# Edge features in one transfer of 128 rows, even and odd tiles, indices three chunks at a time, a written-out SyncE pass

## What is computed

```python
xn = _layernorm(x)
f1 = feature1 @ w_f1a @ w_f1b * gate_edge            # feature1: 54 per edge, gate_edge: 256 per edge
h1 = segment_sum(xn[src] * f1, dst, num_segments=N)
f2 = f1 * gate_edge
h2 = segment_sum(xn[src] * f2, dst, num_segments=N)
...
x = x + gnn(h1, h2, xn) + mix(xn)
x = x + ffn(_layernorm(x))                            # graph attention over 131072 other edges, 4 experts
```

## Time and profile before

| | us |
|---|---|
| median of 3 runs | 1259.7 |
| lowest and highest run | 1254.82, 1261.76 |
| the profiled execution's own time | 1261.14 |
| span of that execution | 1259.1 |
| mean granted TensorE clock | 0.895 of full speed |
| PE busy | 1008.7 (80%) |
| DVE busy | 780.3 (62%) |
| POOL busy | 575.8 (46%) |
| edge pass, first to last filter | 89 to 612 us of the span |

### The profile page before, as it was taken

One profiled execution on the slowest core, in us unless ns is written; L12 is line 12 of the kernel. 1 busy time (PEld: TensorE's weight loads), 2 busy tenths in 40 slices (PEclk: granted clock), 3 DMA queues, 4 the chain that ended last, 5 costly groups with the idle time before them and its releaser, 6 DMA issues.

```text
span 1259.1 us, 14085 instructions
## 1 busy us (share of the span) xinstructions
PE 1008.7 (80%) x3958; PEld 561.8 (45%) x3958; DVE 780.3 (62%) x1487; ACT 420.2 (33%) x832; POOL 575.8 (46%) x578
## 2 busy tenths in 40 slices
PE   4838796978887788888899949858879849969996
PEld 3724342333333333333344438535546525546664
DVE  5636476758667586676568775126546535656388
ACT  3324453544454454453421232121202111212241
POOL 6334656556665656555100000627675735743011
PEclk9968898989989888998999966969889969979998
DMA  9525655656656566566400101000100001011002
GB/s 222 163 64 161 196 180 168 191 181 199 194 180 193 163 191 187 166 192 185 126 34 0 3 19 10 5 2 6 37 6 4 5 3 37 5 4 3 1 16 65
DMA packets 121538, 118.62 MB, mean 94 GB/s; under 512 B 41727, under 2 KB 108939, under 8 KB 121483
## 3 DMA queue, kind: packets, MB, share of 16 engines
q1 hardware_dynamic: 98698, 72.42, 19.7%
q0 software_dynamic: 22784, 45.57, 14.0%
HBM read 112.47 MB, written 5.46 MB: 94 GB/s over the span
## 4 chain that ended last, share of the span: by engine, by line
PE 40%; DVE 23%; another core or an unknown queue 17%; issue 13%; ACT 3%; DVEq 2%; DMA 1%; POOL 1%; SPq 0%; ACTq 0%
PE psum L831 7%; PE psum L960 6%; PE psum L950 5%; PE psum L818 5%; DVE psum L1392 4%; PE psum L929 3%; DVE x_rows L1826 2%; DVE high L1396 2%; DVE high L1702 2%; DVE high L1400 2%; PE psum L864 2%; DVE parts L1692 2%; PE psum L871 2%; PE psum L938 2%
## 5 line engine op out<-in xcount | busy, mean ns | idle before, releaser
L625 POOL DMA_INDIRECT high<-xn_rows,srci x336 | 318.8, 949 | 244.7 <-PE psum L831 105.2
L831 PE MATMUL psum<-high 128*64 128x512 f32 x672 | 212.1, 679 | 4.5 <-issue 3.2
L818 PE MATMUL psum<-filter_weights,shared 54*128 54x256 f32 x672 | 120.3, 440 | 95.0 <-DVE high L1400 75.0
L661 POOL DMA_INDIRECT high<-source_rows,high x104 | 108.4, 1042 | 113.4 <-DVE high L1665 84.1
L960 PE MATMUL psum<-high 128*125 128x256 f32 x640 | 153.1, 396 | 8.8 <-ACT high L1186 6.8
L950 PE MATMUL psum<-xT,high 128*128 (+1 forms) x320 | 144.2, 594 | 10.1 <-issue 10.1
L818 PEld LDWEIGHTS psum<-filter_weights,shared 54*128 54x128 f32 x672 | 71.3, 202 | 180.4 <-DVE high L1400 101.7
L1392 DVE TENSOR_TENSOR psum<-psum,high 128x1024 f32<-128x1024 f32 x96 | 104.8, 1092 | 74.9 <-remote 42.1
L1121 ACT ACTIVATE high<-high 128x1024 f32<-128x1024 f32 x96 | 91.2, 950 | 165.0 <-DVE high L1396 104.9
L960 PEld LDWEIGHTS psum<-high 128*125 128x125 f32 x640 | 126.7, 198 | 36.3 <-ACT high L1186 8.9
L663 POOL DMA_INDIRECT high<-dest_rows,high x104 | 111.6, 1074 | 33.2 <-issue 33.2
(11 more groups left out here) (274 smaller groups left out, 1252.3 us busy)
## 6 DMA issues: line engine op xcount, KB each, us to landing
high<-in_ea SPq DMA_DIRECT2D x48, 896.0 KB
shared<-in_ea SPq DMA_DIRECT2D x96, 108.0 KB
high<-xn_rows,srci POOLq DMA_INDIRECT x336
high<-in_w SPq DMA_DIRECT2D x8, 512.0 KB
x_rows<-in_x SPq DMA_DIRECT2D x5, 448.0 KB
xn_rows<-low SPq DMA_DIRECT2D x5, 448.0 KB
out_rows<-x_rows SPq DMA_DIRECT2D x5, 448.0 KB
high<-source_rows,high POOLq DMA_INDIRECT x104
```

The lines of the kernel that those rows point to most:

```text
L625: pool.indirect_dma_start(gath[j % DEPTH][:, t, :], None, xn_rows_d, bass.IndirectOffsetOnAxis(ap=srci[:, j, t:t + 1], axis=0)).then_inc(s ...
L661: pool.indirect_dma_start(sources[b][:, t, :], None, source_rows_d, bass.IndirectOffsetOnAxis(ap=index[b][:, 0, t:t + 1], axis=0)).then_in ...
L818: ins = pe.matmul(bank[2 + s // 2][:, C * (s % 2):C * (s % 2) + C], feat[j % 2][r:r + 54, slot, :], wf[r:r + 54, :], start=True, stop=True)
L831: ins = pe.matmul(bank[j % 2][g, :], sel[j % 2][:, t, :], msgs[j % DEPTH][:, t, :], start=(t < 2), stop=(t >= CT - 2), skip_group_check=True)
```

## The change

Four edits, all in the edge pass.

1. Features: for chunks 0 to 45 one transfer of 128 rows of 2 KB takes the place of the two of 54 rows. Its source is written as 2 blocks (384 elements apart) of 64 rows of 512 elements: rows 0 to 63 get tiles 0 to 3 of 64 feature rows, rows 64 to 127 tiles 3 to 6. Rows 54 to 63 and 118 to 127 hold values that nothing reads. The last two chunks keep two transfers, now of 54 rows of 2 KB.
2. Halves: the first half of a chunk is tiles 0, 2, 4, 6, the second tiles 1, 3, 5 (before: 0 to 3, and 4 to 6). `filters`, `sums`, the gathers, ACT's square and DVE's three products follow.
3. Indices: one transfer loads the indices of three chunks into one of two halves of `srci`; SP issues it in chunks 2, 5, 8, ..., and POOL waits for indices once in three chunks.
4. SP's pass is written out over all 48 chunks; its addresses are constants.

```diff
-IDX = 6
+IDX3 = 3
+IDX = 2 * IDX3
+TILES = (range(0, CT, 2), range(1, CT, 2))
+HALVES = (slice(0, CT, 2), slice(1, CT, 2))
...
             with sp.Fori(0, npass) as p:
-                with sp.Fori(0, NCH // IDX) as i:
-                    for j in range(IDX):
-                        q = p * NCH + i * IDX + j
-                        c = i * IDX + j
-                        sp.wait_ge(filters_multiplied, q * 2 + 2)
-                        ft = ea54[bass.ds(c, 1)].rearrange("o f t p -> (o f) t p")
-                        for r, first, part in ((0, 0, slice(0, 2)), (64, 1, slice(1, 3))):
-                            sp.dma_start(feat[j % 2][r:r + 54].rearrange("f (a b) p -> f a (b p)", b=2),
-                                         ft[:, first:first + 6, :].rearrange("f (a b) p -> f a b p", b=3)[:, :, part, :]
-                                         .rearrange("f a b p -> f a (b p)")).then_inc(features_loaded[j % 2], 16)
-                        sp.wait_ge(messages_summed, q * 2 + 2)
-                        a = (j + AHEAD) % IDX
-                        sp.dma_start(srci[:, a, :], src[bass.ds(c + AHEAD, 1)].rearrange("o p t -> (o p) t")
-                                     ).then_inc(indices_loaded[a], 16)
-                        sp.dma_start(gate[j % DEPTH], ea256[bass.ds(c, 1)].rearrange("o p (t c) -> (o p) t c", t=CT)
-                                     ).then_inc(gate_loaded[j % DEPTH], 16)
+                for c in range(NCH):
+                    sp.wait_ge(filters_multiplied, p * (2 * NCH) + (2 * c + 2))
+                    if c < NCH - 2:
+                        sp.dma_start(fraw[:, FT * P * (c % 2):FT * P * (c % 2) + FT * P],
+                                     bass.AP(ea54.tensor, 54 * CT * P * c, [[3 * P, 2], [CT * P, 64], [1, FT * P]])
+                                     ).then_inc(features_loaded[c % 2], 16)
+                    else:
+                        for r in range(2):
+                            sp.dma_start(feat[c % 2][64 * r:64 * r + 54], ea54[c][:, 3 * r:3 * r + FT, :]
+                                         ).then_inc(features_loaded[c % 2], 16)
+                    sp.wait_ge(messages_summed, p * (2 * NCH) + (2 * c + 2))
+                    if c % IDX3 == IDX3 - 1:
+                        indices((c // IDX3 + 1) % (NCH // IDX3))
+                    sp.dma_start(gate[c % DEPTH], ea256[c].rearrange("p (t c) -> p t c", t=CT)
+                                 ).then_inc(gate_loaded[c % DEPTH], 16)
...
-                        pool.wait_ge(indices_loaded[j], (p * (NCH // IDX) + i) * 16 + 16)
-                        for h, tiles in enumerate((range(0, 4), range(4, CT))):
+                        if j % IDX3 == 0:
+                            pool.wait_ge(indices_loaded[j // IDX3], (p * (NCH // IDX) + i) * 16 + 16)
+                        for h, tiles in enumerate(TILES):
...
-                for t, r, slot in (((0, 0, 0), (2, 64, 0), (1, 0, 1), (3, 64, 1)),
-                                   ((4, 0, 3), (5, 64, 2), (6, 64, 3)))[h]:
-                    s = t + h
+                for t, r in (((0, 0), (4, 64), (2, 0), (6, 64)),
+                             ((1, 0), (3, 64), (5, 64)))[h]:
+                    s = (t // 2, t // 2 + 5)[h]
...
-                for t in (range(0, 4), range(4, CT))[h]:
-                    g = slice(WIN * (t % 2), WIN * (t % 2) + WIN)
+                for i, t in enumerate(TILES[h]):
+                    g = slice(WIN * (i % 2), WIN * (i % 2) + WIN)
```

More of the change, by code:

```diff
@@ L385, in build @@
         gate_loaded = [sem(f"gate_loaded{i}") for i in range(DEPTH)]
-        indices_loaded = [sem(f"indices_loaded{i}") for i in range(IDX)]
+        indices_loaded = [sem(f"indices_loaded{i}") for i in range(2)]
         features_loaded = [sem(f"features_loaded{i}") for i in range(2)]
@@ L503, in _, with indices @@
                     sp.dma_start(xn_v[b, BW * g:BW * g + BW, :], rows_n[b, BW * g:BW * g + BW, :]).then_inc(rows_stored, 16)
-            for j in range(AHEAD):
-                sp.dma_start(srci[:, j, :], src[j]).then_inc(indices_loaded[j], 16)
+            def indices(g):
+                sp.dma_start(srci[:, IDX3 * (g % 2):IDX3 * (g % 2) + IDX3, :],
+                             src[IDX3 * g:IDX3 * g + IDX3].rearrange("c p t -> p c t")).then_inc(indices_loaded[g % 2], 16)
+            indices(0)
             sp.wait_ge(window_bases_ready, 1)
@@ L807, in _, with filters @@
             npass = pe.value_load(celli[0:1, 0:1], min_val=1, max_val=N // WIN + 1)
-            def filters(q, use, j, h):
+            def filters(p, c, h):
                 if h == 0:
-                    pe.wait_ge(features_loaded[j % 2], use * 32 + 32)
-                pe.wait_ge(messages_ready, q * 2 + (h + 1))
-                for t, r, slot in (((0, 0, 0), (2, 64, 0), (1, 0, 1), (3, 64, 1)),
-                                   ((4, 0, 3), (5, 64, 2), (6, 64, 3)))[h]:
-                    s = t + h
+                    pe.wait_ge(features_loaded[c % 2], p * (8 * NCH + 16) + (c // 2 * 16 + (16 if c < NCH - 2 else 32)))
+                pe.wait_ge(messages_ready, p * (2 * NCH) + (2 * c + h + 1))
+                for t, r in (((0, 0), (4, 64), (2, 0), (6, 64)),
+                             ((1, 0), (3, 64), (5, 64)))[h]:
+                    s = (t // 2, t // 2 + 5)[h]
                     ins = pe.matmul(bank[2 + s // 2][:, C * (s % 2):C * (s % 2) + C],
-                                    feat[j % 2][r:r + 54, slot, :], wf[r:r + 54, :], start=True, stop=True)
+                                    feat[c % 2][r:r + 54, t if r == 0 else t - 3, :], wf[r:r + 54, :], start=True, stop=True)
                 ins.then_inc(filters_multiplied, 1)
@@ L828, in sums @@
                 pe.wait_ge(messages_ready, q * 2 + (h + 3))
-                for t in (range(0, 4), range(4, CT))[h]:
-                    g = slice(WIN * (t % 2), WIN * (t % 2) + WIN)
+                for i, t in enumerate(TILES[h]):
+                    g = slice(WIN * (i % 2), WIN * (i % 2) + WIN)
                     ins = pe.matmul(bank[j % 2][g, :], sel[j % 2][:, t, :], msgs[j % DEPTH][:, t, :],
-                                    start=(t < 2), stop=(t >= CT - 2), skip_group_check=True)
+                                    start=(h == 0 and i < 2), stop=(h == 1 and i >= 1), skip_group_check=True)
                 ins.then_inc(messages_summed, 1)
@@ L846, in _ @@
                 for h in range(2):
-                    filters(p * NCH, p * (NCH // 2), 0, h)
+                    filters(p, 0, h)
                 for c in range(NCH):
@@ L850, in _ @@
                         if c + 1 < NCH:
-                            filters(p * NCH + (c + 1), p * (NCH // 2) + (c + 1) // 2, c + 1, h)
+                            filters(p, c + 1, h)
                         sums(p * NCH + c, c, h)
@@ L1117, in square @@
             def square(p, c, h):
-                ts = (slice(0, 4), slice(4, CT))[h]
+                ts = HALVES[h]
                 act.wait_ge(first_messages_ready, (p * NCH + c) * 2 + (h + 1))
@@ L1379, in _ @@
             v0 = st.base + st.k
-            halves = (slice(0, 4), slice(4, CT))
+            halves = HALVES
             banks = (psum[:, 2:4, :].rearrange("p b (t c) -> p (b t) c", c=C),
```

## The result

The changed kernel takes 1281.28 us (median of 4 runs, 1272.9 to 1283.35), the kernel before 1259.99 beside it (1254.82 to 1261.76). The ratio is 1.0163, 95% interval 1.0109 to 1.0218: slower by 1.6%. The profiled execution's own time is 1280.72 us, its span 1278.9 (before: 1261.14 and 1259.1).

A forecast was written before the change was run, and what follows sets the result against it. PE and DVE waiting for each other, not any load, were taken to bound the edge pass; terms 0 + 0 + 0 + 3 gave +3 us on 1261.14, which is 1264, so 1263 us for a median, range 1250 to 1292.

The forecast's parts named there:

- the likeliest case: Edge pass: the work of the two DMA engines fits within a chunk; 1257 to 1269 us around 1263, chance 0.46.
- the two engines saturate: Rival, edge pass: two DMA engines need more than the 11.0 us a chunk takes; 1278 to 1296 us, chance 0.30.
- No load sets the pace before: Edge pass of the kernel before: loads arrive several us early, so remote waits lie between PE and DVE.
- SP's pass written out, the halves: Edge pass: earlier gate issues gain 0; wider operand spacing from even and odd tiles costs 0, bound -3 to +3 us.
- Their work, 10.3 to 12.0 us a chunk, of which I took 10.3 to 10.9: Edge pass: load of the two DMA engines carrying features, with gate, gathers and indices, against 11.0 us a chunk.
- That fits, barely: Edge pass: the two DMA engines' 10.3 to 10.9 us of work stays within the 11.0 us a chunk takes.
- 3 us for quick chunks that follow each other: Edge pass: in successive chunks of 8 to 9 us the two engines fall back 2 us each; +3 us in all.
- Indices: late, but covered: POOL's gathers: may wait some 2 us in 15 groups, cost 0; rival, uncovered: up to 45 us, chance 0.05.
- The gate lands 10.4 us after its issue: Edge pass, gate transfer behind features on the two engines: lands within the shortest lead of 12.7 us.
- a chunk over 11.3 us: Sign of saturation in the edge pass; without saturation the chunk was to take 11.0 to 11.1 us.
- A longer remote wait ahead of the first product: Sign of saturation: DVE waits longer "remote" before a chunk's first product, line 1392 before the change.
- A fifth of the waits goes with fewer packets: Rival: with features on 16 engines, a fifth of PE's 75.0 us wait goes; -15 us, 1245 us, chance 0.14.

The follow-up runs named there:

- e11: The kernel before with the source of its feature transfers written as 2 blocks of 27 rows; packet count stayed the same; 1052.32 us, ratio 0.9996.
- e1: The changed kernel with its one feature transfer split into two of 64 rows of 2 KB; 1051.29 us, ratio 0.9989 to the kernel before.
- e9: The changed kernel, unchanged, run on another chip where the kernel before is quick; 1147.87 us, ratio 1.0901 to the kernel before.
- e4: The changed kernel with indices loaded as before, one chunk at a time and two ahead; 1148.93 us, ratio 1.0925 to the kernel before.
- e10: The changed kernel with indices loaded as before, one chunk at a time, two ahead, repeated on another quick chip; 1149.41 us, ratio 1.0927.
- e8: The changed kernel with features in two transfers of 57 rows, carried by three engines, on the slow chip; 1247.99 us, ratio 1.0016 to the kernel before.
- e5: The kernel before, unchanged, run again for a trace on the slow chip; 1246.84 us, ratio 0.9995.

## Why the prediction came out as it did

1263 us was predicted, 1250 to 1292 the range; 1281 is in it, but above the likeliest case (1257 to 1269) and beside the rival "the two engines saturate" (middle value 1278, chance 0.30). That the rival's number is so near is luck: it takes 11.6 us of work a chunk against a mean of 11.0, while 10.86 were measured, with which its own sum gives no loss at all.

- *No load sets the pace before:* held. In e11 DVE waits for no DMA ahead of line 1392, and e1, with 16 engines for 9 on the features, gives 0.9989.
- *SP's pass written out, the halves: 0.* Held, e1; the product of line 1402 keeps 1087 ns.
- *Their work, 10.3 to 12.0 us a chunk, of which I took 10.3 to 10.9:* held. 10.86 us was measured, with a slope of 0.074 us a packet over the wide step and 0.085 to 0.093 over the narrow one.
- *"That fits, barely", and 3 us for quick chunks that follow each other:* **this is the step that failed**, a term of the right mechanism with the wrong size. I held 10.3 to 10.9 against the mean chunk of 11.0 us. The mean hides that half of the chunks are shorter than the engines need. Replayed on the 47 chunk lengths of the trace before: the engines fall behind by 10.86 less the chunk's length, catch up in long ones, and what exceeds the spare lead is lost. That gives 52 us with no spare lead, 24 us with 2.3 us of it, 18 us with 3 and none with 6. I had the lead in hand, a gate that lands 10.4 us after issue against a shortest lead of 12.7, so 2.3 us. The 24 us that follow stand beside 21 and 17 measured, where I had put 3. This is a calculation after the fact; what the runs show is the floor of 10.86 on the A chips, and on B that three engines undo the loss.
- *Indices: late, but covered.* POOL waits 45.0 us in 10 places, where I had expected some 2 us in 15; in e9 they land 15.5 us after issue in the median, where I had 5.4. Its cover held on the A chips (e4, e10); on B it wasn't separated.
- *The gate lands 10.4 us after its issue:* sized for one chunk without a backlog. Where the two engines are always behind, it is 17.0 us (e9), and the gate costs more than the features do: DVE waits 93.0 us for it, PE 69.5 us for them.
- *What would show it:* a chunk over 11.3 us came (11.38), though the sign was meant for engines that need more than 11.0. A longer remote wait ahead of the first product hardly did (42.1 to 47.0 us); it went to line 1432 (56.6 to 68.9) and to PE (75.0 to 83.4). Apart from POOL's indices, the trace of the changed kernel names a load as the cause of a wait only for PE's filters, 8.7 us in 3 places; the A chips' traces had to name it.
- *A fifth of the waits goes with fewer packets:* not so. On B, with three engines and 5860 packets fewer (e8), PE waits 84.0 us for DVE's last product where the kernel before waits 77.6 (e5), and the ratio is 1.0016. The remote waits come with the chip.

## What to carry to other kernels

Merging two transfers into one can take engines away: compare the outermost counts of both sides, here 2 and 128, before counting what an issue saves. By their completions, two transfers of 64 rows ran on 16 engines each, one of 128 on two. Hold the work of the fullest DMA engine, all queues together, against the shortest chunks and the spare lead, not against the mean chunk; and don't take a small loss on one chip for a small cost, since a chip on which the pass waits elsewhere hides most of it.

## What I had not expected of the hardware

- The kernel before took 1052 us on two chips, 1247 and 1260 us in the other two measurements, with "remote" waits of DVE of up to 10 us in the pass in the latter only, each ahead of line 1422 some 5 to 13 us after the recorded end of the product that it waits for. The change costs 9.0% where the kernel is quick (9.2% on the other such chip, with early indices) and 1.5 to 1.6% where it is slow.
- One row more in a transfer, 59 for 58, cost 212 us, 4.44 us in each chunk.
- A backlog on two DMA engines holds up SP while it issues: 2.9 us in the median for a gate transfer (e9) where 0.55 is usual.
